# Making the list of an expert's rows two tiles ahead, inside the expert stage, instead of all eight ahead of it

## The reference

```python
xf = x.reshape(N, D)                                   # N = 4096 tokens, D = 256
route_prob = jax.nn.softmax(xf @ Ws + bs, axis=-1).T   # E = 8 experts
route_vals, routes = jax.lax.top_k(route_prob, k)      # k = N / E = 512 tokens an expert
xin = xf[routes]
h = jax.nn.gelu(jnp.einsum('ekd,edf->ekf', xin, W1) + b1[:, None, :])   # F = 1024
out = jnp.einsum('ekf,efd->ekd', h, W2) + b2[:, None, :]
out = out * route_vals[..., None]
final = jnp.zeros((N, D)).at[routes.reshape(-1)].add(out.reshape(-1, D))
```

## Time and profile before

| | us |
|---|---|
| median of 3 runs | 2802.72 (2800.18 to 2804.92) |
| profiled execution | 2806.87 |
| its span, from the first to the last instruction | 2805.1 |
| list stage, from its first comparison to its last entry | 336.30 to 403.81 |
| first expert stage, TensorE's first to last matmul | 415.15 to 649.8 |
| mean granted clock of TensorE | 0.898 of 2.4 GHz |

### The profile page before, as it was taken

How to read it: one execution, slowest core, us unless ns; L and a number is a source line. 1 busy time by engine, 2 the same in 40 slices (tenths; PEclk the granted TensorE clock), 3 DMA queues, 4 the chain that set the end, 5 groups by cost and what they waited for, 6 DMA issues and landing times. The chain is left out here.

```text
span 2805.1 us, 39165 instructions
## 1 busy us (share of the span) xinstructions
PE 2312.8 (82%) x10904; PEld 1292.5 (46%) x10904; DVE 1332.8 (48%) x3459; ACT 1020.3 (36%) x1827; POOL 737.5 (26%) x764
## 2 busy tenths in 40 slices
PE   6793119994899999999679989989945999999991
PEld 2462116762233344333223333333324888888880
DVE  3555661112666666666257767766736111111114
ACT  2230002120355555555326555555620322332322
POOL 0110012333311222210132333223220433333335
PEclk9885559997899999999769999999977999999995
DMA  4220014434523332332043343234202666666654
GB/s 140 100 68 22 0 58 115 118 85 105 66 35 51 55 47 41 46 52 27 22 46 47 54 55 48 38 47 54 32 16 92 180 182 188 181 186 184 188 155 129
DMA packets 196358, 235.26 MB, mean 84 GB/s; under 512 B 21538, under 2 KB 177698, under 8 KB 195682
## 3 DMA queue, kind: packets, MB, share of 16 engines
q1 hardware_dynamic: 174498, 202.90, 31.7%
q0 software_dynamic: 21696, 30.42, 6.1%
HBM read 146.23 MB, written 35.91 MB: 65 GB/s over the span
## 5 line engine op out<-in xcount | busy, mean ns | idle before, releaser
L1569 DVE CUSTOM_DVE_ANT_0 atL1x_junk<-atL1x_pm,bias 128x512 bf16<-128x512 f32 x512 | 345.5, 688 | 229.0 <-PE atL1x_pm L1249 227.4
L1565 DVE TENSOR_REDUCE atL_tops<-atL_pm 128x1 f32<-128x512 f32 x512 | 339.6, 684 | 186.3 <-PE atL_pm L1249 183.0
L1406 ACT ACTIVATE atL1x_prob<-atL1x_ps 128x512 f32<-128x512 f32 x512 | 303.7, 598 | 291.3 <-PE atL1x_ps L1266 282.5
L878 PE MATMUL exL_ph<-exL_xgT,exL_w 128*128 128x256 f32 (+1 forms) x1504 | 395.5, 419 | 6.0 <-ACT exL_hid L901 3.6
L888 PE MATMUL exL_po<-exL_w,exL_hid 128*128 128x256 f32 x1760 | 392.2, 382 | 8.0 <-ACT exL_hid L901 4.1
L1406 ACT ACTIVATE atL_prob<-atL_ps 128x512 f32<-128x512 f32 x512 | 294.9, 599 | 263.0 <-PE atL_ps L1263 259.8
L888 PEld LDWEIGHTS exL_po<-exL_w,exL_hid 128*128 128x128 f32 x1760 | 330.5, 190 | 61.9 <-issue 18.5
L901 ACT ACTIVATE exL_hid<-exL_ph,exL_b 128x256 f32<-128x256 f32 (+1 forms) x376 | 190.1, 511 | 421.0 <-PE exL_ph L878 376.5
L878 PEld LDWEIGHTS exL_ph<-exL_xgT,exL_w 128*128 128x128 f32 x1504 | 276.0, 191 | 114.6 <-issue 61.5
L847 POOL DMA_INDIRECT sum<-exL_ys,exL_put x110 | 178.1, 1619 | 464.8 <-DVE exL_ys L936 259.3
L909 DVE COPY exL_xgT<-exL_pt 128x256 f32<-128x256 f32 (+1 forms) x98 | 41.8, 469 | 387.2 <-PE exL_pt L867 270.0
(11 more groups left out here) (308 smaller groups left out, 2741.8 us busy)
## 6 DMA issues: line engine op xcount, KB each, us to landing
exL_w<-in_L_W SPq DMA_DIRECT2D x94, 1024.0 KB, 4.9
atL1x_kstack<-atL1x_k SPq DMA_DIRECT2D x96, 128.0 KB, 4.6
atL1x_qstack<-atL1x_q SPq DMA_DIRECT2D x96, 128.0 KB, 6.6
atL_kstack<-atL_k SPq DMA_DIRECT2D x96, 128.0 KB, 4.6
atL_qstack<-atL_q SPq DMA_DIRECT2D x96, 128.0 KB, 7.0
exL_b<-in_L_b SPq DMA_DIRECT2D x47, 128.0 KB, 5.9
sum<-tok_zero SPq DMA_DIRECT2D x1, 4224.0 KB, 15.3
aft_ctxT<-in_ctxT SPq DMA_DIRECT2D x2, 2048.0 KB, 10.5
```

Of the source, the lines that this page charges most:

```text
L878: mm = pe.matmul(ph[f % 2][:], w1[slot][:, m, f * P:(f + 1) * P], xgT[:, m, :], start=m == 0, stop=m == DC - 1)
L1406: act.activation(prob[i % PROBS][:], ps[i % 2][:], ACT.Exp, scale=SCALE).then_inc(s["p_ready"], 1)
L1565: ins = dve.tensor_reduce(tops[g % 2][:, t, j:j + 1], pm[i % TOPS][:], AX.X, ALU.max)
L1569: ins = dve.tensor_tensor_reduce(junk[:, i % TOPS, :], pm[i % TOPS][:], G["bias"][0][:, t, :], 1.0, -BIG / 2, ALU.add, ALU.max, tops[g % 2 ...
```

## The change

The eight lists are no longer made in one stage. `first_lists` makes only the first two (`FIRST = 2`), in straight code without a loop, and enters each into `row` and `roww` by itself. The buffers live in `EarlyLists` and stay through the expert stage. In tile t, for t from 0 to 5, VectorE first makes the two slabs of expert t+2 (`list_ahead`), TensorE adds up the first after four of its eight groups of the first layer and the second after the eighth, in a PSUM tile of its own, `plist`, and VectorE then enters the list. GpSimd waits for that (`entered`) before it fetches the rows of tile t+2. Tiles 6 and 7 run as before, in a loop of their own (`run_lists`). The operations of a slab and their shapes are those of before; an entry is six operations on one expert's 20 sums instead of all 160.

```diff
+FIRST = 2
...
+    def slab(self, dve, G, chain, built, r, s):
...
+        chain(dve.tensor_tensor(self.hot_low[s][:], G["lane"][:].unsqueeze(1).broadcast_to([P, SLAB, P]),
+                                chunks(self.lowf[:, here], P), ALU.is_equal))
+        chain(dve.tensor_tensor(self.hot_high[:], G["lane"][:, 0:cols].unsqueeze(1).broadcast_to([P, SLAB, cols]),
+                                chunks(self.highf[:, here], cols), ALU.is_equal))
+        first = s * SLAB % NC
+        for n, (scale, by_token) in enumerate(self.tables):
+            rows_ = slice(first, first + SLAB) if by_token else here
+            dve.tensor_tensor(self.scaled[s][:, :, n, :], self.hot_high[:], chunks(scale[:, rows_], cols),
+                              ALU.mult).then_inc(built, 1)
+
+    def sum_slab(self, pe, pt, s):
+
+        for i in range(SLAB):
+            mm = pe.matmul(pt[:, 0:self.PARTS * self.COLS], self.hot_low[s][:, i, :],
+                           self.scaled[s][:, i, :, :].rearrange("p k c -> p (k c)"),
+                           start=s == 0 and i == 0, stop=s == self.SLABS - 1 and i == SLAB - 1)
+        return mm
...
+    def enter(self, dve, G, chain, pt, r):
+
+        cols, here = self.COLS, bass.ds(r * self.COLS, self.COLS)
+        chain(dve.tensor_copy(self.sums[:].rearrange("p k c -> p (k c)"), pt[:, 0:self.PARTS * cols]))
+        chain(dve.tensor_reduce(self.total[:, 0], self.sums[:, 0:2, :].rearrange("p k c -> p c k"), AX.X, ALU.add))
+        chain(dve.tensor_reduce(self.total[:, 1], self.sums[:, 2:, :].rearrange("p k c -> p c k"), AX.X, ALU.add))
+        chain(dve.tensor_scalar(self.spare[:], self.total[:, 0], 0.0, G["spare1"][:, 0:1], ALU.is_equal, ALU.mult))
+        chain(dve.scalar_tensor_tensor(out=G["row"][:, here], in0=self.total[:, 0], scalar=-1.0, in1=self.spare[:],
+                                       op0=ALU.add, op1=ALU.add))
+        return dve.tensor_copy(G["roww"][:, here], self.total[:, 1])
...
+                for r in range(FIRST):
+                    for s in range(SLABS):
+                        if r:
+
+                            dve.wait_ge(summed, past(r * SLABS))
+                        early.slab(dve, G, chain, built, r, s)
+                        dve.wait_ge(built, past((r * SLABS + s + 1) * PARTS))
+                for r in range(FIRST):
+                    dve.wait_ge(summed, past((r + 1) * SLABS))
+                    early.enter(dve, G, chain, pt[r], r).then_inc(entered, 1)
+                    dve.wait_ge(entered, past(r + 1))
+
+            @block.tensor
+            def _(pe):
+                for r in range(FIRST):
+                    for s in range(SLABS):
+                        pe.wait_ge(built, past((r * SLABS + s + 1) * PARTS))
+                        early.sum_slab(pe, pt[r], s).then_inc(summed, 1)
...
+        def run_lists(eng, tile, first=0):
+
+            for begin, end, with_list in ((first // 2, (tiles - FIRST) // 2, True), ((tiles - FIRST) // 2, tiles // 2, False)):
+                with eng.Fori(begin, end) as pair:
+                    tile(pair * 2, 0, pair, with_list)
+                    tile(pair * 2 + 1, 1, pair, with_list)
...
+                    if with_list:
+                        pool.wait_ge(entered, past(t + 1))
+                        alone(pool)
                     fetch(t + 2, slot)
...
+                        if with_list and f % (FC // early.SLABS) == FC // early.SLABS - 1:
+                            part = f // (FC // early.SLABS)
+                            pe.wait_ge(built, past((t * early.SLABS + part + 1) * early.PARTS))
+                            if part == 0:
+                                pe.wait_ge(entered, past(t))
+                            early.sum_slab(pe, plist, part).then_inc(summed, 1)
 
                     turn_rows(1 - slot, pair + slot)
...
+                def list_ahead(t):
+
+                    chain = Chain(dve, lchain, t * LPER)
+                    for part in range(early.SLABS):
+                        dve.wait_ge(summed, past(t * early.SLABS))
+                        alone(dve)
+                        early.slab(dve, G, chain, built, t + FIRST, part)
+                    dve.wait_ge(summed, past((t + 1) * early.SLABS))
+                    alone(dve)
+                    early.enter(dve, G, chain, plist, t + FIRST).then_inc(entered, 1)
+                    assert chain.n == LPER
+
+                def tile(t, slot, pair, with_list=False):
+                    if with_list:
+                        list_ahead(t)
                     dve.wait_ge(turned, past(t + 2))
...
-        lists(nc, G, "L0", E, NC, CAP // P, True)
-        experts(nc, G, a, "L0", ACT.Gelu_apprx_tanh)
+        with ExitStack() as keep:
+            early = EarlyLists(nc, keep)
+            first_lists(nc, G, early)
+            experts(nc, G, a, "L0", ACT.Gelu_apprx_tanh, early)
```

More of the change, by code:

```diff
@@ new lines, in first_lists, with _ @@
+def first_lists(nc, G, early):
+    with ExitStack() as ctx:
+        st = Stage(nc, ctx, "liL0")
+        n_all, I32 = E * NC, mybir.dt.int32
+        whole, high, low = (st.sb(n, [P, n_all], I32) for n in ("whole", "high", "low"))
+        place_in, rest = st.sb("place_in", [P, 1]), st.sb("rest", [P, n_all])
+        pt = [st.ps(f"pt{i}", [P, S]) for i in range(FIRST)]
+        vchain, built, summed, entered = (st.sem(n) for n in ("vchain", "built", "summed", "entered"))
+        SLABS, PARTS = early.SLABS, early.PARTS
+        with nc.Block() as block:
+            @block.sync
+            def _(sp):
+                st.set_semaphores(sp)
+                st.retire(sp, G["tok_sems"])
+            @block.vector
+            def _(dve):
+                chain = Chain(dve, vchain)
+                chain(dve.tensor_copy(whole[:], G["place"][:, 0:n_all]))
+                chain(dve.tensor_scalar(high[:], whole[:], 7, None, ALU.logical_shift_right))
+                chain(dve.tensor_scalar(low[:], whole[:], P - 1, None, ALU.bitwise_and))
+                chain(dve.tensor_copy(early.highf[:], high[:]))
+                chain(dve.tensor_copy(early.lowf[:], low[:]))
+                chain(dve.tensor_scalar(G["row"][:], G["spare1"][:].broadcast_to([P, COLS]), -1.0, None, ALU.add))
+                chain(dve.memset(G["roww"][:], 0.0))
+                chain(dve.tensor_scalar(place_in[:], G["spare1"][:], -float(N), None, ALU.add))
+                chain(dve.tensor_scalar(early.chunk_at[:], G["token1"][:], place_in[:, 0:1], None, ALU.subtract))
+                chain(dve.tensor_copy(early.within[:], place_in[:].broadcast_to([P, NC])))
+                weight, wparts = G["weight"][:, 0:n_all], early.wparts
+                chain(dve.tensor_copy(wparts[0][:], weight))
+                chain(dve.tensor_tensor(rest[:], weight, wparts[0][:], ALU.subtract))
+                chain(dve.tensor_copy(wparts[1][:], rest[:]))
+                chain(dve.tensor_tensor(rest[:], rest[:], wparts[1][:], ALU.subtract))
+                chain(dve.tensor_copy(wparts[2][:], rest[:]))
+                for r in range(FIRST):
[14 more added lines that the diff above has]
+                        early.sum_slab(pe, pt[r], s).then_inc(summed, 1)
@@ L742, in _, with experts @@
                         mm.then_inc(summed, 1)
-def experts(nc, G, a, tag, gelu):
+def experts(nc, G, a, tag, gelu, early=None):
     rows, sums, tiles, size = G["rows" + tag[1]], G["sum" + tag[1]], TILES[tag], TILES_OF[tag]
@@ L759, in experts @@
         hid, ys = st.sb("hid", [P, FC, size]), [st.sb(f"ys{i}", [P, TC, D]) for i in range(2)]
+        if early:
+            plist = st.ps("plist", [P, S])
+            built, summed, entered, lchain = (st.sem(n) for n in ("built", "summed", "entered", "lchain"))
+            LPER = early.SLABS * 2 + early.ENTRY
         shift = st.sb("shift", [P, D]) if tag == "L1" else None
@@ L823, in fetch @@
                         ).then_inc(gathered[slot], 16)
-                def tile(t, slot, pair):
+                def tile(t, slot, pair, with_list=False):
                     pool.wait_ge(gathered[slot], (pair + 1) * TC * 16)
@@ L852, in _ @@
                 fetch(1, 1)
-                tile(0, 0, 0)
-                tile(1, 1, 0)
-                run(pool, tile, 2)
+                tile(0, 0, 0, bool(early))
+                tile(1, 1, 0, bool(early))
+                if early:
+                    run_lists(pool, tile, 2)
+                else:
+                    run(pool, tile, 2)
                 for sem in added:
@@ L890, in tile @@
                         mm.then_inc(out_ps, 1)
-                run(pe, tile)
+                if early:
+                    run_lists(pe, tile)
+                else:
+                    run(pe, tile)
             @block.scalar
@@ L937, in tile @@
                                           ALU.mult).then_inc(ys_ready, 1)
-                run(dve, tile)
+                if early:
+                    run_lists(dve, tile)
+                else:
+                    run(dve, tile)
```

18 lines of the change are left out of this document (added).

## The result

The changed kernel takes 2766.32 us (median of 4 runs, 2761.50 to 2769.19), the kernel before 2803.47 (4 runs, 2800.18 to 2804.92): ratio 0.9863, 95% interval 0.9843 to 0.9883. The prediction was 2770.8. The profiled execution took 2763.92 us, its span is 2762.1. Lines have moved: the first layer's matmuls are L1011, the transposes L1000, the second layer L1027, the burst L673, the comparison L660, the first and last operation of the entry L683 and L689, the output product L1089 and L1092, GpSimd's copies L943 (`get`) and L967 (`put`), its gathers L947 and scatters L977.

A forecast was written before the change was run, and what follows sets the result against it. TensorE bounds the kernel as a whole, VectorE's chain the list stage. -49.5 + 0.2 + 6.6 + 10.8 = -31.9 us from the median 2802.72 gives 2770.8; range 2757 to 2785.

The forecast's parts named there:

- Part 1: List stage: six lists leave it, gain 49.5 us (bounds 48.5 and 50); four more semaphores before GpSimd's first gather cost 0.2.
- Part 2: First layer of six tiles: two bursts of 16 small matmuls each, 0.55 us a burst, 6.6 us in all.
- Part 3: Second layer of six tiles: TensorE waits through entry, gather, put copy and product, 1.8 us with restart, 10.8 in all.
- A: Rival: no wait in the second layer because the put copy comes in time; -42.7 us, 2760; chance 0.14.
- B: Rival: same chain but longer, 4.5 us a tile; -22.3 us, 2780; chance 0.20 together with C.
- C: Rival: VectorE late at the first burst, 1.5 us a tile, 9 us more, 2780; chance 0.20 together with B.
- D: Rival: each tile's new wait drops TensorE's clock to 1.2 GHz; 126 us, 2897, slower than before; chance 0.03.
- the other case that part 3 allowed for: Expert tiles: a scatter holds VectorE for its 1.6 us; the first slab then comes at 6.8, still before 6.9.
- The sum: List and expert stages together: -49.5 + 0.2 + 6.6 + 10.8 = -31.9 us, median 2770.8.
- don't change: Stages behind the expert stage: they start from the landing of the last scatter and keep their lengths.

The follow-up runs named there:

- e1: The changed kernel, but GpSimd copies tile t's piece into `put` before it waits for the new list: 2757.40 us, ratio 0.9832.
- e4: All eight lists made ahead in straight code, six made again in the tiles into unread scratch, GpSimd not waiting for them: 2807.91 us, ratio 1.0020 to the kernel before.
- e5: As e4, but GpSimd waits for the scratch list before it gathers, as in the changed kernel: 2824.64 us, ratio 1.0065 to the kernel before.
- c3: The kernel before, unchanged, in a third profiled execution: 2807.76 us (one run).
- e2: The changed kernel, but TensorE adds up the second slab after six of its eight first-layer groups instead of after the eighth: 2761.38 us, ratio 0.9845.
- e7: The kernel of e1 with one list made ahead; the second is made while GpSimd gathers the first expert's rows: 2749.14 us, ratio 0.9804.
- e3: The changed kernel, but all eight lists made ahead in straight code and none in the tiles: 2812.53 us, ratio 1.0031 to the kernel before.

## Why the prediction was right, step by step

**Part 1** (-49.5, +0.2): measured 355.75 - 338.57 = 17.2 us against 67.5, so -50.3. A slab in straight code is 341.95 - 338.57 = 3.38 us, where I took 3.7. The four more semaphores cost nothing up to GpSimd's copy: from entry to copy it is 0.53 us as before. (The fives of the clock line, which I placed around 280 to 420 us, begin at 210, in the choice; nothing hangs on it.)

**Part 2** (6.6): mis-sized. A burst takes 411.79 - 411.38 = 0.41 us from its start to the next matmul's; the 0.15 that I put on top for the weight load is in no run. A listed tile without the wait is 29.35 us (`e1`, `e4`) against 28.67: 0.68 a tile, not 1.1, so 4.1 us in six. In `e1` the first layer with its bursts is 0.89 longer than before (14.63 against 13.74), the step from transposes to second layer 0.11 shorter and the second layer 0.10 shorter. The pitch did not halve with the clock: 0.41/16 is 26 ns for 20 columns. This agrees with the floor of 25 ns that the Trainium skill gives ("TensorE: Matmul & The Clock Gate", section "Wait — 56ns, not 53.3ns?").

**Part 3** (10.8): right in its mechanism and nearly in its size. From the tile's start at 404.52, predicted and measured: second burst over 14.9, 14.8; list entered 17.0, 16.65; GpSimd awake 17.3, 16.8; `put` copied 23.4, 22.85; product done 24.5, 23.95; TensorE asks at 22.8, 22.6. The wait was 1.40 us here, and 8.6 in six, 1.4 a tile instead of 1.7; GpSimd woke 0.13 us after the entry, where I took 0.3. But the second to sixth tile take (559.98 - 404.52)/5 = 31.09 us each, 29.35 without the wait, so 1.74 a tile for a mean idle time of 1.48: the restart costs 0.26, where I took 0.1. The two errors nearly cancel, which is luck, and 10.3 us (`e1`) or 10.0 (`e5` against `e4`) stand for the 10.8.

One sum of part 3 is wrong. From its own figures GpSimd is free 25.3 + 4.6 + 4.6 + 8.2 + 1.55 - 31 = 13 us into the next tile, not 11, and the room ahead of the list is 4 us, not 6. The forecast did not need it. Measured, the last scatter of this tile ends at 444.95 + 1.55 = 446.50, 11.0 into the next tile, and the room is 5.7: the last scatter came 6.4 us after its predecessor, not 8.2.

A term that I hadn't: the first tile costs 3.5 us more (404.52 - 370.65 = 33.87 against 448.93 - 418.58 = 30.35), not 2.4. Its matmuls start at the half clock in both kernels, and it stayed there longer after the change. The second three microseconds of the tile's first layer, before (clock 0.97) and after (0.52), and last in the third execution of the kernel before, `c3` (0.50):

```profile
421.60:424.60 3.00, 3.00 (x8) 1.21 (x8) 0.00 (x0) 1.37 (x2) 1.22 (x3) 0.97 1.07 359
```

```profile
373.70:376.70 3.00, 3.00 (x5) 1.03 (x4) 2.72 (x6) 0.69 (x1) 0.00 (x0) 0.52 1.09 363
```

```profile
426.82:429.82 3.00, 3.00 (x4) 1.06 (x4) 0.00 (x0) 0.69 (x1) 1.23 (x3) 0.50 1.08 364
```

So the longer stay at half clock comes without the change too: the first tile of `c3` took 31.73 us, those of the other two executions of that kernel 30.35 and 30.30. The two of the changed kernel took 33.87 and 33.80, of which a listed tile's usual 2.4 is the change's; the rest is within what the kernel before does by itself.

**The rivals.** A (no wait) is refuted by the six waits, and `e1` is what A would have been: 2757.40 against A's 2760. B (4.5 us a tile) by the tile's 2.4. C: no idle time stands ahead of a burst. D: from the first tile's transposes on the granted clock is 1.00 in every window to the end of the listed tiles, across all six waits of 1.2 to 1.5 us.

Scatters were held by comparisons, but by 0.8 us at most in the changed kernel and 2.1 in `e2` (3.68 us instead of 1.56), and TensorE lost nothing by it (every tile of `e2` but the first takes 29.64 or 29.65). Held were only those that began while a comparison was running. First the changed kernel, comparison and scatter, then `e4`, where the scatter began 0.25 us ahead of the comparison:

```profile
405.60 2.29 DVE L660 TENSOR_TENSOR early_hot_low<-lane,early_lowf 128x2048 bf16<-128x2048 f32 x1
...
407.48 1.85 POOL L977 DMA_INDIRECT sum<-exL_ys,exL_put  x1 [2.95 <-DMA sum<-exL_ys,exL_put]
```

```profile
452.54 1.56 POOL L976 DMA_INDIRECT sum<-exL_ys,exL_put  x1 [3.01 <-DMA sum<-exL_ys,exL_put]
...
452.79 2.28 DVE L661 TENSOR_TENSOR early_hot_low<-lane,early_lowf 128x2048 bf16<-128x2048 f32 x1
```

The five scatters of the changed kernel's trace that began beside a running comparison end 1.43 or 1.44 us after its end (here 409.33 against 407.89). The five of `e4` that began first took 1.55 to 1.66, about as alone, and the comparison kept its 2.28 to 2.29: VectorE was not held, the other case that part 3 allowed for. The Trainium skill ("SBUF — State Buffer", section "Who interferes with whom") infers that descriptor generation isn't held by tensor_tensor. These scatters, and the gather of 346.90 in `e7`, which took 2.16 where the one of 352.35, alone, took 0.95, decide against that inference for an indirect DMA. Such an instruction also reads its row numbers from SBUF, and the traces don't tell which part of it was held.

**The sum**: the two stages gave -35.4 against -31.9. Of the 3.5 us between them 2.3 are in the expert stage, mostly the bursts, and 1.2 in the list stage. The median came 4.5 below the forecast; the last 1.0 of that no trace places. Against it stands a loss that I said wouldn't be, since the stages behind "don't change". In every kernel with the new code the stretch from `top_experts` to the second expert stage is 1.5 to 4.3 us longer than the 72.3 of before. In the first trace of each kernel VectorE's timeline is the same up to its last list entry; then TensorE waits longer for the first gathered rows. Before:

```profile
2149.82 1.14 POOL L820 DMA_INDIRECT exL_xg<-rows,exL_get  x1 [0.96 <-SPq L71]
...
2156.60 1.12 PE L867 MATMUL exL_pt<-ident,exL_xg 128*128 128x128 f32 x4 [10.15 <-DMA exL_xg<-rows,exL_get]
```

After:

```profile
2104.85 1.14 POOL L947 DMA_INDIRECT exL_xg<-rows,exL_get  x1 [1.42 <-SPq L71]
...
2112.78 1.12 PE L1000 MATMUL exL_pt<-ident,exL_xg 128*128 128x128 f32 x4 [11.77 <-DMA exL_xg<-rows,exL_get]
```

The gather starts 0.46 us later behind GpSimd's copy, and its rows come 1.15 later still. In `e3` that wait is 10.17, as before, and the extra 2.4 us stand ahead of GpSimd's copy, so it isn't one place that grew. Why is open; no experiment was made on it.

## What to carry to other kernels

Work that is taken off one engine's stretch and put beside another engine's can cost more by what its signals hold up than by what it computes: here 3 to 4 us of matmuls and 10 us of one wait, which was only the order of two things in GpSimd's queue. When a wait is added, look at what stands behind it in the same queue and move ahead what doesn't need it; then ask whether the next piece can leave the stretch too (`e7`). And before a difference of 10 us is explained, see whether it lies in a stage that was touched.

## What the runs showed of the hardware that I had not expected

- With the same instructions at the same times within 0.02 us over the 35 us before, TensorE's granted clock fell from 1.00 to 0.50 in one execution, some 1 us after an idle time of 0.67 us, and stayed at 1.00 in another (`e4` and its repetition). Over the second attention such falls make up to 14.3 us, more than the wait that was studied.
- In the listed tiles idle times of 1.2 to 1.5 us, twice that length, leave it at 1.00 every time.
- An indirect DMA that GpSimd begins to issue while a VectorE tensor_tensor with two inputs in SBUF is running ends only 1.43 to 1.44 us (scatters of the changed kernel) or 0.85 to 1.13 us (gathers of `e7`) after that instruction's end: 1.68 to 2.34 instead of 1.56, and 2.16 and 2.69 instead of 0.95. One that began 0.25 to 0.81 us ahead of the tensor_tensor was not held (`e4`: 1.55 to 1.66 us), nor was VectorE (2.28 to 2.29 us).
